# Reading cached keys with indirect DMAs in every attention unit, in place of page copies made ahead

## The reference

```python
x = x + L0(x)   # gate/up/down projection, 512 -> 1376 -> 512, silu, with low-rank factors per sequence
x = x + L1(x)   # attention over a paged cache, below
x = x + L2(x)   # weight quantised with an 8-entry codebook, then x @ w.T
x = x + L3(x)   # one of 8 weights by adapter id
# L1: 32 query heads, 8 key heads, D = 128, 16 pages of 32 tokens per sequence
q, k, v = (rmsnorm+rope of x@Wq), (rmsnorm+rope of x@Wk), x @ Wv
kc = k_cache[block_table].reshape(8, 512, 8, 128)      # k_cache is (64 pages, 32, 8 heads, 128)
vc = v_cache[block_table].reshape(8, 512, 8, 128)
probs = softmax(mask(q @ concat(kc, k).T * scale));  o = probs @ concat(vc, v);  x + o @ Wo.T
```

## Time and profile before

| | |
|---|---|
| median of 3 runs | 1540.37 us (1539.57 to 1541.89) |
| the profiled execution | 1541.23 us |
| its span, first to last instruction | 1539.6 us |
| TensorE busy | 94% of the span |
| VectorE, ScalarE, GpSimd busy | 76%, 61%, 34% |
| granted TensorE clock, mean | 0.981 |

### The profile page before, as it was taken

How to read it: one execution, slowest core, us unless ns; L and a number is a source line. 1 busy time by engine, 2 the same in 40 slices (tenths; PEclk the granted TensorE clock), 3 DMA queues, 4 the chain that set the end, 5 groups by cost and what they waited for, 6 DMA issues and landing times.

```text
span 1539.6 us, 29405 instructions
## 1 busy us (share of the span) xinstructions
PE 1443.9 (94%) x8014; PEld 1239.8 (81%) x8014; DVE 1164.8 (76%) x2800; ACT 937.9 (61%) x1860; POOL 518.2 (34%) x726
## 2 busy tenths in 40 slices
PE   3997999789999999999999998999899999999978
PEld 2775788568888788878888887888788888888767
DVE  4675776357888688878877887888778878888756
ACT  2332332247777667767766776777677667777643
POOL 6444440033333333333333333333334333333200
PEclk9997999899999999999999999999999999999999
DMA  9887882401021112111111111121112111111214
GB/s 190 281 239 263 268 254 77 147 14 56 29 70 42 50 29 69 42 51 48 43 60 39 54 58 50 35 63 42 50 35 63 59 40 49 42 49 35 97 59 161
DMA packets 104275, 131.03 MB, mean 85 GB/s; under 512 B 11861, under 2 KB 79590, under 8 KB 98838
## 3 DMA queue, kind: packets, MB, share of 16 engines
q1 hardware_dynamic: 97142, 103.19, 21.5%
q0 software_dynamic: 6560, 24.23, 5.1%
q10 hardware_dynamic: 384, 1.41, 0.6%
HBM read 125.63 MB, written 36.72 MB: 105 GB/s over the span
## 4 chain that ended last, share of the span: by engine, by line
PE 82%; DVE 6%; issue 5%; ACT 2%; DMA 2%; SPq 1%; POOL 0%; ACTq 0%; DVEq 0%; POOLq 0%
PE proj_ps L1167 17%; PE sc L1207 14%; PE o_ps L1244 13%; PE proj_ps L1265 12%; PE ring L1226 9%; PE sc L1023 4%; PE proj_ps L1023 4%; PE o_ps L1023 4%; PE ring L1280 2%; PE ring L1292 2%; PE ring L1023 1%; SPq L322 1%; DVE w_l L1423 1%; DVE pTl L1704 1%; DMA prep<-scale_dram 1%
## 5 line engine op out<-in xcount | busy, mean ns | idle before, releaser
L1704 DVE TENSOR_TENSOR pTl<-ring,pTh 128x512 fp32r<-128x512 f32 x320 | 215.2, 689 | 72.2 <-ACT pTh L848 68.4
L637 POOL TENSOR_TENSOR rstd<-var,half_neg 128x4 f32<-128x4 f32 x64 | 79.7, 1245 | 546.0 <-DVE var L1741 489.3
L830 ACT ACTIVATE p_sb<-p_sb,bias,rstd 128x640 f32<-128x640 f32 x256 | 235.7, 921 | 42.4 <-DVE bias L1680 42.4
L848 ACT ACTIVATE pTh<-ring 128x512 fp32r<-128x512 f32 x320 | 184.5, 599 | 56.4 <-PE ring L1226 55.6
L1670 DVE CUSTOM_DVE_ANT_0 p_sb<-sc,mask 128x640 f32<-128x640 f32 x256 | 209.1, 817 | 5.7 <-PE sc L1207 2.0
L1226 PE MATMUL ring<-ident,p_sb 128*128 128x128 f32 x1280 | 183.7, 275 | 7.1 <-DVE p_sb L1696 4.5
L1167 PE MATMUL proj_ps<-wh,xh 128*128 128x512 f32 (+1 forms) x512 | 179.7, 351 | 6.8 <-issue 6.1
L1226 PEld LDWEIGHTS ring<-ident,p_sb 128*128 128x128 f32 x1280 | 153.8, 141 | 35.3 <-DVE p_sb L1696 3.7
L1167 PE MATMUL proj_ps<-wl,xh 128*128 128x512 f32 (+1 forms) x512 | 172.6, 337 | 0.0
L1167 PE MATMUL proj_ps<-wh,xl 128*128 128x512 f32 (+1 forms) x512 | 172.1, 336 | 0.0
L1207 PE MATMUL sc<-kTh,qTh 128*128 128x320 f32 x512 | 163.8, 320 | 2.6 <-DVE kTl L1805 2.6
(11 more groups left out here) (248 smaller groups left out, 3695.4 us busy)
## 6 DMA issues: line engine op xcount, KB each, us to landing
v_pages<-in_v_cache POOLq DMA_DIRECT2D x128, 128.0 KB, 3.8
k_raw<-k_pages SPq DMA_DIRECT2D x64, 256.0 KB, 3.0
v_raw<-v_pages SPq DMA_DIRECT2D x64, 256.0 KB, 2.9
stage<-in_Wqkv SPq DMA_DIRECT2D x32, 384.0 KB, 3.4
w_raw<-in_WguT SPq DMA_DIRECT2D x20, 512.0 KB, 6.9
k_pages<-in_k_cache SPq DMA_DIRECT2D x80, 128.0 KB, 4.4
stage<-in_WoT SPq DMA_DIRECT2D x32, 256.0 KB, 3.3
w_raw<-in_W3T SPq DMA_DIRECT2D x8, 1024.0 KB, 5.3
```

The lines of the kernel that those rows point to most:

```text
L830: act_e.activation(p_sb[:, p_slot(u, h), :], p_sb[:, p_slot(u, h), :], ACT.Exp, bias=bias[:, h:h + 1], scale=rstd[:, u.k % 2, h:h + 1], ac ...
L848: act_e.activation(pTh[:, c, :], ring[c % 2][:, :], ACT.Copy).then_inc(S["pth"], 1)
L1704: v.tensor_tensor(pTl[:, c, :], ring[c % 2][:, :], pTh[:, c, :].bitcast(F32), ALU.subtract).then_inc(S["ptl"], 1)
```

## The change

The key copies and `k_pages` go. POOL reads the keys of each unit itself, with four indirect DMAs (one for each 128 cached tokens) from a table of row numbers `key_row`, one row number for each partition, which it counts up by one when a sequence goes to its next head. VectorE makes the first table once (`key_rows`). The value copies wait for the progress of the feed-forward stage, eight for each block. Parts of the quantised weight, the last `store_group` and the copies of turned sequences stand later.

```diff
-SP_PAGES = 5 * NPP
+PARTS = {1: ((1, 2),), 2: ((1, 3), (1, 4)), 3: (), 4: ((2, 0), (2, 1)), 5: ((2, 2), (2, 3)), 6: ((2, 4),), 7: (),
+         8: ((3, 0), (3, 1)), 9: ((3, 2), (3, 3)), 10: ((3, 4),)}
# SP
-                copy_keys(3)                      # and copy_keys(4), copy_keys(2) in the later loops
-                if q == CH + 4:
+                if q == CH + 5:
                     store_group(1)
                     load_group(2)
-                if q == CH + 8:
+                if q == CH + 9:
                     store_group(2)
                     load_group(3)
-            store_group(3)
             for n in range(FC):
                 if n >= 3:
                     load_wd(CH + n)
-                copy_keys(2)
-
+                if n == 3:
+                    store_group(3)
                 if n == 2:
                     sp.wait_ge(S["gate_up"], 4 * FC)
                     load_wqkv(first, 0)
                     load_wqkv(first, 1)
-                    load_k(first)
             def step(u):
-                if u.exists() and (u.turn is not None or u.k > 0):
-                    load_k(u)
# POOL
+            pool.dma_start(prep[:, 7, 0:P].bitcast(I32), ins["pages"]...partition_broadcast(P)).then_inc(S["pages_in"], 16)
+            # and two small iotas
-            copy_values(0, B * NPP)               # and the loop with POOL's 48 key copies
+            for n in range(16):
+                pool.wait_ge(S["gate_up"], 2 * n + 1)
+                copy_values(8 * n, 8 * n + 8)
+            def gather_k(u):
+                if not u.exists():
+                    return
+                for c in range(LC):
+                    pool.indirect_dma_start(
+                        out=k_raw[:, c, :], out_offset=None, in_=ins["k_cache"].rearrange("a s h d -> (a s h) d"),
+                        in_offset=bass.IndirectOffsetOnAxis(ap=key_row[:, u.seq, c:c + 1], axis=0)).then_inc(S["k_load"], 16)
+            def next_head(u):
+                if not u.exists():
+                    return
+                pool.wait_ge(S["k_load"], u.count(LC * 16, LC * 16))
+                pool.wait_ge(S["kcT"], u.count(1, 1))
+                pool.tensor_tensor(key_row[:, u.seq, :], key_row[:, u.seq, :], one_i[:, :], ALU.add).then_inc(S["row_next"], 1)
             def step(u):
                 turn_and_norm(u)
                 split_v(u + -1)
+                next_head(u)
+                gather_k(u + 1)
+            pool.wait_ge(S["gate_up"], 4 * FC)
+            gather_k(Unit(None, 0))
# ACT
-                if n == 4 or n == 9:
+                if n == 4 or n == FC - 1:
                     copy_delta(n // 9)
-            act_e.wait_ge(S["w2_put"], 16 * C)
             for k in range(2, CH):
                 split_wd(CH + k)
+                if k == 4:
+                    act_e.wait_ge(S["w2_put"], 16 * C)
-                if k in (4, 6, 8, 10):
+                if k in (5, 7, 9, 11):
                     high_x1(k // 2 - 2)
# TensorE: the four delta(g) products one or two blocks later; transpose_keys waits for all four gathers
-                pe.wait_ge(k_load, u.count(16, 16))
+                pe.wait_ge(S["k_load"], u.count(LC * 16, LC * 16))
# VectorE: key_rows() at block 3 (11 small instructions), weight2(1, 0) at block 10 instead of 9,
# weight2(1, 1) and all later parts after it as in PARTS, low_x1 as high_x1
-                else:
-                    weight2(*divmod(n - 4, 5))
+                    key_rows()
+                elif n < 9:
+                    weight2(0, n - 4)
+                elif n == FC - 1:
+                    weight2(1, 0)
```

More of the change, by code:

```diff
@@ L167, in cond_resid_kernel @@
         idx = keep("idx", [1, B * NPP + 2 * B], I32)
+        key_row = keep("key_row", [P, B, LC], I32)
+        one_i = keep("one_i", [P, LC], I32)
         l0 = ExitStack()
@@ L360, in load_wd @@
                 load(wd_raw[0:rows(n), r % 3, :], ins["WdT"][n * P:n * P + rows(n), :], wd_in[r % 3])
[L362 to L371, removed]
             def load_group(g):
@@ L417, in _ @@
             load_wd(3)
-            copy_keys(3)
             sp.wait_ge(S["xl_set"], 2 * C)
@@ L437, in of_head @@
                 return v[:, :, bass.ds(u.head * D, D)]
[L439 to L444, removed]
             def load_v(u):
@@ L542, in _ @@
             pool.dma_start(nw[:, 1, :], ins["kw"].partition_broadcast(P)).then_inc(S["nw_in"], 16)
+            pool.dma_start(prep[:, 7, 0:P].bitcast(I32), ins["pages"].rearrange("b n -> (b n)").partition_broadcast(P)
+                           ).then_inc(S["pages_in"], 16)
+            pool.iota(one_i[:, :], pattern=[[0, LC]], base=1, channel_multiplier=0).then_inc(S["iota_set"], 1)
+            pool.iota(prep[:, 7, P:P + 1].bitcast(I32), pattern=[[0, 1]], base=0, channel_multiplier=HK).then_inc(S["iota_set"], 1)
             pool.iota(pos_i[:, :], pattern=[[0, B]], base=0, channel_multiplier=1).then_inc(S["iota_set"], 1)
@@ L791, in _ @@
                 high_act(FC + m - 1)
-                if m == 2 or m == 6:
-                    copy_delta(2 + m // 6)
+                if m == 4 or m == 8:
+                    copy_delta(1 + m // 4)
                 if m < FC - 1:
@@ L1123, in _ @@
                     lora_down(n - 1)
-                if n == 1 or n == 8:
-                    delta(n // 8)
+                if n == 1 or n == 9:
+                    delta(n // 9)
             down(0, 0)
@@ L1142, in _ @@
                     down(0, m + 2)
-                if m == 1 or m == 5:
-                    delta(2 + m // 5)
+                if m == 3 or m == 7:
+                    delta(1 + m // 3)
             for k in range(CH):
@@ L1468, in _, with key_rows @@
             v.tensor_copy(key, key_i).then_inc(S["key_copied"], 1)
+            def key_rows():
+                dve.wait_ge(S["pages_in"], 16)
+                page, row = prep[:, 8, 0:P], prep[:, 8, P:P + 1]
+                v.tensor_copy(row, prep[:, 7, P:P + 1].bitcast(I32))
+                then(v.tensor_copy(page, prep[:, 7, 0:P].bitcast(I32)))
+                for n in range(4):
+                    part = slice(n * PSIZE, (n + 1) * PSIZE)
+                    i = v.tensor_scalar(page[part, :], page[part, :], float(PSIZE * HK), -float(n * PSIZE * HK), ALU.mult, ALU.add)
+                then(i)
+                then(v.tensor_scalar(page, page, row, None, ALU.add))
+                for n in range(4):
+                    part = slice(n * PSIZE, (n + 1) * PSIZE)
+                    i = v.tensor_copy(key_row[part, :, :], page[part, :].rearrange("p (b c q) -> p b c q", b=B, q=4)[:, :, :, n])
+                i.then_inc(S["row_set"], 1)
             def masks():
@@ L1604, in _ @@
             low_t(1, 0)
-            weight2(1, 2)
+            weight2(1, 1)
             mask_t(1, 1)
@@ L1615, in _ @@
                 split_wd(m + 3)
-                if m == 1:
-                    weight2(1, 3)
-                    weight2(1, 4)
-                elif m == 2:
-                    weight2(2, 0)
-                elif m == 3:
-                    weight2(2, 1)
-                    weight2(2, 2)
-                elif m < 6:
-                    weight2(2, m - 1)
-                else:
-                    weight2(3, m - 6)
+                for part in PARTS[m]:
+                    weight2(*part)
                 if m == FC - 1:
```

16 lines of the change are left out of this document (4 added, 12 removed).

## The result

Slower: 1629.4 us median of 4 runs (1627.71 to 1630.76), against 1539.97 for the kernel before beside it; the ratio is 1.0586, 95% interval 1.0568 to 1.0603. The forecast was 1525.5, in a range of 1512 to 1585. The span went from 1539.6 to 1626.1, by 86.5 us, and two stages made it.

The account below looks back on a forecast made before the run. Attention was taken as bound by TensorE, busy 155.80 of 156 us. From 1541.23 us, minus 21.3 won in the feed-forward stage, plus 6.4 lost where the loop turns, gives 1526.3; the median 0.86 lower, 1525.5; range 1512 to 1585.

Parts of the forecast that it names:

- I take X = 1.0: Attention, POOL: each of a unit's four key gathers was taken to hold POOL for 1.0 us.
- the sum 5.97 against 6.04: Ordinary attention unit: addition 0.37, gathers 4.0 and tail 1.6 make 5.97 us, just fitting the 6.04 before TensorE turns keys.
- the tail from the last issue's start: Attention: from the end of the last gather's issue to its landing, 1.6 us, between 1.2 and 2.6; X comes before it.
- 0.54 from below: Lower bound on X: a DMA from POOL to 128 partitions holds it for 0.54 us, without reading row numbers.
- gathers too slow: Rival, chance 0.28: chain exceeds 6.04 us, TensorE waits at transpose_keys every unit; 25 us per 0.1 on X; slower, 1584 at 1.25.
- The estimate of 2.15 from the last issue: Attention: the skill's figure for a 64 KB gather's landing, 2.15 us from the last issue, making the chain 5.5.
- POOL's q_sin moves to 506.8: Attention: q_sin moves from 503.49 to 506.8, still in time; k_sin about 1.2 us later, free until X reaches about 1.15.
- VectorE holds the gathers up (0.05): Rival, chance 0.05: each gather lets a VectorE instruction of 0.69 us pass; chain 2.8 longer, 179 us lost, 1698.
- The feed-forward stage: 21.3 us: Total won from shorter TensorE holes in that stage: 1.24 + 2.92 + 2.1 + 15 = 21.3 us, between 9.5 and 27.
- The hole of 7.31: Feed-forward, block 10: TensorE's wait gets 2.1 us shorter as four fewer instructions stand between down split and gated(10).
- The stretch at the end: End of the feed-forward stage: 48 us becomes 33, 15 won, as block 5 is split ahead of the turned sequence.
- SP's loop: End of the feed-forward stage: SP's weight loads and the splits they wait for take an estimated 8.1 us per two blocks.

Follow-up runs that it names:

- a4: e6 with two gathers in a unit instead of four: 1566.4 us, ratio 1.017.
- e4: Changed kernel with four plain POOL DMAs in place of the indirect ones, same place, page table ignored: 1553.7 us, ratio 1.008.
- e12: Kernel before the change, with only the copies of the turned sequences one block later: 1529.1 us, ratio 0.993.
- e2: Changed kernel with two key buffers, gathers in the same place but for the unit after next: 1624.4 us, ratio 1.054.
- e6: Changed kernel with SP reading the keys, page table ignored, and the four gathers in their place filling a buffer nobody reads: 1620.4 us, ratio 1.053.
- e1: Changed kernel with the address addition and the gathers moved ahead of rstd of q: 1518.0 us, ratio 0.986.
- e5: e2 with the address addition and gathers moved ahead of rstd of q, as in e1: 1520.0 us, ratio 0.988.
- e7: Changed kernel with SP reading the keys, page table ignored, and four POOL additions of 128x512 at the gathers' place: 1624.4 us, ratio 1.056.
- e8: Changed kernel without gathers, two key buffers, SP reading keys for the unit after next behind its value load, page table ignored: 1517.8 us, ratio 0.986.
- a5: e6 with four gathers of 32 rows each in place of 128: 1668.8 us, ratio 1.085.
- e10: Changed kernel unedited, on another chip: 1638.2 us, ratio 1.063.
- a1: Changed kernel unedited, a third time, on another chip: 1635.3 us, ratio 1.062.

## Why the prediction was wrong

**The failed step: "I take X = 1.0", and with it the sum 5.97 against 6.04.** The chain and the price of being late were the right model; it came out at 7.18. The terms: 0.37 for the addition was 0.32; the tail from the last issue's start, X + 1.6 = 2.6, was 2.53 and 0.12; but the three distances between gathers, 3.0 in the sum, were 1.35 + 1.27 + 1.59 = 4.21. That is the whole error of 1.2 us. X as the duration of one was fine, 0.978 in the median. What the sum left out is that the next one starts 0.30 us after the end of the last, and that the third takes up to 1.31 beside VectorE's q_cos, as it did in 40 of 64 units. The bound "0.54 from below" came from a group whose row showed durations alone, while for the page copies I had both, duration and address reading. The Trainium skill (Perfetto Trace Analysis, "GPSIMD Engine Instruction") says to time GpSimd's instructions by the spacing of their starts; that is what the rows show.

**The rival "gathers too slow"** named this mechanism and gave 25 us for each 0.1 on X. By its formula an excess of 1.14 makes 57 x 1.14 + 6 x 2.2 = 78 us, and 1597 in all. The other 32 us lie in part in the 26.7 us more that the same products took, which the lower clock explains in part, and where I took every unit that isn't a turn for an ordinary one: those with weight splits lose up to 2.6, the turns 2.9, and twice POOL stood still for over 4 us. The two accounts overlap and I haven't separated them. I gave it 0.28, and cut its range off at X = 1.25.

**"The tail 1.6, between 1.2 and 2.6"**: right, 2.53 less 0.95.

**The estimate of 2.15 from the last issue** (the Trainium skill, DMA: Bandwidth & Descriptors, Anatomy of one DMA): the trace of the changed kernel shows 2.4 to 2.9, with a median of 2.55. Its chain of 5.5 missed the distances as mine did.

**"POOL's q_sin moves to 506.8 ... it costs nothing until X reaches about 1.15".** Half right. In the changed kernel VectorE waits 2.08 for k_sin in a unit (143.9 us in 61 waits), but behind a TensorE that is already late for the keys. What this sentence lacked is shown by a4 and e4: a POOL that starts q_sin 2 to 3 us later runs it beside VectorE's q_cos and stretches both. Even with the short X of e4, 0.56 each, the kernel would have been at 1553.7, not at 1525.5.

**"VectorE holds the gathers up (0.05)"**: only one of four gathers in a unit, by 0.35 us, not each by 0.69.

**The feed-forward stage: 21.3 us, measured 23.9.** The hole of 7.31 lost 2.08 (2.1 predicted). The stretch at the end is 33.7 us (33 predicted), though not by SP's loop as I had it. The terms of that loop add up to 8.6, not the 8.1 that I wrote, which would make 34.6. And e12, with SP's copies in place, wins nearly as much by the order of the splits. Up to that stretch 9.7 were won where I had 6.3. The holes alone give 5.0 of them, a new one of 0.91 counted in. What I left out is the granted clock: before, it fell to its lower level (0.50, 1.2 GHz) within the holes of 2.92 and of 7.31 and stayed there for 17.0 us in all; after, only for 3.4, from the hole of 5.24 on (windows, before and then after):

```profile
119.60:126.40 6.80, 5.97 (x14) 4.72 (x15) 2.92 (x6) 1.98 (x4) 2.93 (x6) 0.50 0.93 332
133.30:143.50 10.20, 5.86 (x14) 4.64 (x15) 8.55 (x15) 4.27 (x8) 4.29 (x9) 0.50 0.54 145
```
```profile
127.90:131.30 3.40, 3.04 (x7) 2.48 (x8) 3.40 (x8) 2.92 (x6) 1.26 (x3) 0.50 0.30 92
```

At 0.50, 11.8 us of products hold what takes 5.9 at 1.00, and 3.0 what takes 1.5: an estimated 4.4 us won. The range of 9.5 to 27 holds.

**What it comes to.** The chain of gathers and landing was too long, and in the changed kernel's first trace its end is what TensorE waited for (85.4 us). But in the old place, with this wait taken away, as much is lost all the same: e2 and e6 show late signals there. Where POOL is held for a shorter time, its q_sin runs beside VectorE's q_cos, which is part of e4's 37 us and of a4's loss; the changed kernel doesn't have that cost. Only leaving the place takes all of it away (e1, e5).

**What stays open.** What makes the signals late. They come only with indirect DMAs, on all four chips of the experiments and not in the trace of the changed kernel's own measurement; not with plain DMAs from POOL (e4), POOL arithmetic (e7) or SP's transfers (e8); with 32 rows as with 128. That they are the whole of what e2 and e6 lose is read from the waits; no run takes them away alone. And gathers in the old place with keys in time were never seen with signals on time, so it isn't shown that the landing is the whole of the loss in the first measurement.

## What to carry to other kernels

When work is put on an engine, cost it by the distance from start to start, and walk through what the engine did next: which engine was idle or busy beside it then, and which is now. Before moving work ahead of a consumer, look for the wait that the engine has in any case: POOL's 6.7 to 8 us before q_var held the same four gathers for nothing, 7% faster than 10 us later in the same step. When taking a wait away wins nothing, the place may have a second cost of the same size behind the first.

## What the runs showed of the hardware

- An indirect DMA of 128 rows of 512 bytes holds POOL for 0.98 us in the median, and the next starts 0.30 behind its end, 1.25 to 1.34 from start to start, and 1.59 where the first of the two ran beside VectorE's q_cos. With 32 rows it is 0.86 and 1.17 (a5). A plain one from POOL takes 0.54, and the next starts after 0.53 (e4).
- From the start of the last of four gathers to landing it took 2.4 to 2.9 us.
- While gathers run, some TensorE semaphore updates can come 0.5 to 3.3 us late, some 190 of 1100, at fixed distances from the gathers. Of three traces of one program two show it (e10, a1) and one doesn't (1 update).
- VectorE's q_cos, 0.68 alone, took 1.24 in the median beside POOL's q_sin (a4) and 1.77 beside POOL's additions (e7). Beside a gather it kept 0.68, and the gather took up to 1.31 in place of 0.95.
